# Moving the low part of a split from VectorE to TensorE and ScalarE in a Mamba scan (one core)

## What is computed

```python
A = -jnp.exp(A_log)
xp = jnp.einsum('bld,rd->blr', x, x_proj_w)
dt_in, B, C = ...
dt = jax.nn.softplus(jnp.einsum('blr,dr->bld', dt_in, dt_proj_w) + dt_proj_b)
dA = jnp.exp(dt[..., None] * A)
dBx = dt[..., None] * B[:, :, None, :] * x[..., None]
def step(h, inp):
    dA_t, dBx_t, C_t = inp
    h = dA_t * h + dBx_t
    y = jnp.einsum('bdn,bn->bd', h, C_t)
    return (h, y)
y = ys + D * x
```

## Time and profile before

| what | value |
|---|---|
| time, median of 3 runs | 844.35 us (841.13, 844.35, 847.69) |
| the profiled execution's own time | 841.76 us |
| its span in the profile | 840.0 us |
| busy in the span: PE / DVE / ACT / POOL | 779.4 / 620.4 / 439.4 / 307.7 us |
| the scan stage, from the first scan to the sum of the last product | 26.85 to 194.96 us |

### The profile page before, as it was taken

The page is one execution under the profiler, slowest core; times in us unless marked ns, Lnnn a source line. Parts: engine busy times, 40 slices in busy tenths (PEclk is TensorE's granted clock), DMA queues, the critical chain, the costliest instruction groups (busy, mean ns, idle before and its releaser), DMA issues.

```text
span 840.0 us, 18994 instructions
## 1 busy us (share of the span) xinstructions
PE 779.4 (93%) x7930; PEld 368.7 (44%) x7930; DVE 620.4 (74%) x879; ACT 439.4 (52%) x594; POOL 307.7 (37%) x235
## 2 busy tenths in 40 slices
PE   8758787797999999999999999999988999999997
PEld 2434344445444444444343444444424544444444
DVE  3999999997565333456759999999966787774344
ACT  4987767645754330143237788788895533332100
POOL 0799898992003000058402223222342122221000
PEclk9599999999999999999999999999999999999999
DMA  6900000005230000039900000000052033310011
GB/s 215 387 4 2 4 3 2 4 4 176 100 112 8 1 0 1 1 57 194 151 1 2 2 3 3 2 2 2 23 164 62 1 119 126 120 63 0 13 38 51
DMA packets 53296, 46.62 MB, mean 56 GB/s; under 512 B 38289, under 2 KB 44241, under 8 KB 53218
## 3 DMA queue, kind: packets, MB, share of 16 engines
q1 hardware_dynamic: 53218, 45.49, 18.8%
HBM read 34.87 MB, written 2.16 MB: 44 GB/s over the span
## 4 chain that ended last, share of the span: by engine, by line
PE 70%; DVE 15%; issue 5%; ACT 5%; POOL 2%; DMA 1%; SPq 1%; DVEq 0%; ACTq 0%; POOLq 0%
PE ps L906 13%; PE ps L670 10%; PE ps L647 9%; PE ps L828 8%; DVE arena L1462 7%; PE ps L942 7%; PE ps L749 6%; PE ps L726 6%; PE ps L805 4%; DVE arena L1686 2%; PE ps L753 2%; PE ps L561 1%; POOL arena L1296 1%; PE ps L515 1%; ACT arena L1195 1%
## 5 line engine op out<-in xcount | busy, mean ns | idle before, releaser
L1686 DVE TENSOR_REDUCE arena<-ps 128x1 f16<-128x512 f32 (+3 forms) x320 | 183.4, 630 | 16.6 <-PE ps L749 8.0
L1195 ACT ACTIVATE arena<-ps 128x1024 f32<-128x1024 f32 (+2 forms) x160 | 143.6, 942 | 36.6 <-PE ps L805 33.7
L1296 POOL TENSOR_TENSOR arena<-arena 128x1024 f32<-128x1024 f32 x62 | 145.5, 2377 | 12.1 <-DVE arena L1462 10.0
L1462 DVE TENSOR_TENSOR_SCAN arena<-arena,ps 128x1024 f32<-128x1024 f32 x64 | 141.9, 2270 | 0.8 <-PE ps L561 0.5
L906 PE MATMUL ps<-arena 128*128 128x512 f16 x528 | 114.6, 379 | 0.1
L670 PE MATMUL ps<-arena 128*128 128x512 f16 (+1 forms) x464 | 97.6, 372 | 1.0 <-ACT arena L1115 1.0
L749 PE MATMUL ps<-arena 64*128 64x512 f16 (+3 forms) x384 | 91.8, 329 | 3.3 <-DVE arena L1686 1.3
L561 PE MATMUL ps<-arena 64*128 64x64 f16 x3072 | 58.9, 194 | 33.5 <-DVE arena L1462 32.7
L647 PE MATMUL ps<-arena 128*128 128x512 f16 x384 | 88.8, 383 | 0.0
L561 PEld LDWEIGHTS ps<-arena 64*128 64x128 f16 x3072 | 51.1, 97 | 82.7 <-DVE arena L1462 78.2
L1354 POOL TENSOR_SCALAR_AFFINE_SELECT arena<-arena 128x512 f32<-128x512 f32 x64 | 42.0, 664 | 123.1 <-ACT arena L1195 122.9
(11 more groups left out here) (180 smaller groups left out, 968.9 us busy)
## 6 DMA issues: line engine op xcount, KB each, us to landing
arena<-in_w_q_dram SPq DMA_DIRECT2D x11, 768.0 KB, 4.1
arena<-c_rows SPq DMA_DIRECT2D x16, 512.0 KB, 10.7
arena<-in_w_s_dram SPq DMA_DIRECT2D x11, 384.0 KB, 4.9
arena<-in_x_fm_dram SPq DMA_DIRECT2D x8, 256.0 KB, 4.4
out_dram<-arena SPq DMA_DIRECT2D x8, 256.0 KB, 2.0
arena<-in_wg_dram SPq DMA_DIRECT2D x1, 1792.0 KB, 10.2
arena<-in_wu_dram SPq DMA_DIRECT2D x1, 1792.0 KB, 7.3
arena<-in_wd_dram SPq DMA_DIRECT2D x1, 1792.0 KB, 11.3
```

What stands on the lines that cost most here:

```text
L1195: nc.scalar.activation(dst, src, ACT.Exp, scale=float(HD) ** -0.5).then_inc(exp_done, 1)
L1296: nc.gpsimd.tensor_tensor(hC[i % 4][:], hst[i % 3][:], c_all[:, n, :], ALU.mult).then_inc(hc_done, 1)
L1462: nc.vector.tensor_tensor_scan(hst[i % 3][:], dA[i % 3][:], banks(2 * (i % 2), 2), 0.0, ALU.mult, ALU.add).then_inc(scan_done, 1)
L1686: nc.vector.reduce_max(maxima_slot(half, k), ps[:, ring_bank(n), 0:len(heads) * w].rearrange("p (a w) -> p a w", a=len(heads)), AX, negate ...
```

## The change

PE subtracts the high part from the turned product by a matmul with a negated identity in f16, accumulating in PSUM (`cut_high`: two matmuls of 128 x 512, behind the sum of n = 12, in chunk 0 of n = 13), and ACT copies what is left to f16 (`tok_low`, now on ACT, behind dA of n = 13, in chunk 0 of n = 14); DVE's `tok_low` is gone. For chunks 2 and 3, `make_dt` part 2 on DVE is gone too: PE adds max(z, 0) by a matmul with the f32 identity (`add_positive`: two matmuls of 128 x 512, behind the sum of n = 9), once part 1 has signalled. Chunk 1 keeps part 2 on DVE. The negated identity takes the place of `ident_h` and is made by one DVE instruction near the start. The transposes carry a start flag only on the first of the four in a bank.

```diff
--- before.py
+++ after.py
@@ -168,6 +168,7 @@
         picks_b = small("picks_b", [P, 2, P], bf16)
         b_parts = [x[:].rearrange("p s n -> p (s n)").bitcast(f32).rearrange("p (q n) -> p q n", q=TT) for x in (mask_b, picks_b)]
         ident_h = small("ident_h", [P, P], f16)
+        negative = ident_h
         skips = small("skips", [P, DC, SUB])
         ld_tab, tables_made = sem("ld_tab"), sem("tables_made")
         q_proj, k_proj, v_proj = sem("q_proj"), sem("k_proj"), sem("v_proj")
@@ -345,6 +346,7 @@
         b_kept, b_turned, b_high, diag_built, ident64_made = (
             sem("b_kept"), sem("b_turned"), sem("b_high"), sem("diag_built"), sem("ident64_made"))
         b_low, b_copied = sem("b_low"), sem("b_copied")
+        negative_made, tok_cut, log_joined = sem("negative_made"), sem("tok_cut"), sem("log_joined")
         diag_by_act, diag_by_pool = sem("diag_by_act"), sem("diag_by_pool")
         ACT_PIECES = {2: (6, 0), 3: (6, 1), 4: (8, 0), 5: (8, 1), 8: (11, 0), 9: (11, 1), 10: (14, 0), 11: (14, 1)}
         POOL_PIECES = {1: (7, 0), 3: (7, 1), 5: (12, 0), 7: (12, 1), 9: (15, 0), 11: (15, 1)}
@@ -528,8 +530,28 @@
                 if c:
                     pe.wait_ge(dt_done, whole(c))
                 for q in qs:
-                    last = nc.tensor.transpose(ps[:, TURN_BANK[c] + q // 4, (q % 4) * P:(q % 4 + 1) * P], dtx[:, q * P:(q + 1) * P], ident_sb[:])
+                    last = nc.tensor.matmul(ps[:, TURN_BANK[c] + q // 4, (q % 4) * P:(q % 4 + 1) * P], dtx[:, q * P:(q + 1) * P], ident_sb[:],
+                                            start=(q % 4 == 0), stop=True, is_transpose=True, skip_group_check=True)
                 last.then_inc(dtx_turned, 1)
+
+            def add_positive(c):
+
+                pe.wait_ge(log_joined, c - 1)
+                pe.wait_ge(z_pos, c)
+                for h in range(2):
+                    last = nc.tensor.matmul(banks(DT_BANK[c] + h, 1), ident_sb[:], dtx[:, h * HALF:(h + 1) * HALF],
+                                            start=False, stop=True, skip_group_check=True)
+                last.then_inc(dt_joined, 1)
+
+            def cut_high(c):
+
+                pe.wait_ge(tok_high_done, whole(c))
+                pe.wait_ge(negative_made, 1)
+                for h in range(2):
+                    last = nc.tensor.matmul(banks(TURN_BANK[c] + h, 1), negative[:],
+                                            dtx_tok[c % 2][:, 0, 4 * h:4 * h + 4, :].rearrange("p q d -> p (q d)"),
+                                            start=False, stop=True, skip_group_check=True)
+                last.then_inc(tok_cut, 1)
 
             def residual(c):
 
@@ -591,6 +613,10 @@
                     for lag in SUM_LAGS[c > 0].get(n, (LAG,)):
                         if i >= lag:
                             add_y(i - lag)
+                    if c + 1 < DC and n == (12 if c else 13):
+                        cut_high(c + 1)
+                    if 1 <= c < DC - 1 and n == 9:
+                        add_positive(c + 1)
             for n in range(NS - LAG, NS):
                 add_y((DC - 1) * NS + n)
 
@@ -1001,6 +1027,11 @@
 
                 act.wait_ge(dtx_turned, whole(c))
                 nc.scalar.copy(dtx_tok[c % 2][:, 0].rearrange("p q d -> p (q d)"), banks(TURN_BANK[c], 2)).then_inc(tok_high_done, 1)
+
+            def tok_low(c):
+
+                act.wait_ge(tok_cut, c)
+                nc.scalar.copy(dtx_tok[c % 2][:, 1].rearrange("p q d -> p (q d)"), banks(TURN_BANK[c], 2)).then_inc(tok_low_done, 1)
 
             def take_y(c):
 
@@ -1062,6 +1093,8 @@
                         keep_dt(c + 1)
                     if c + 1 < DC and n == (12 if c else 13):
                         tok_high(c + 1)
+                    if c + 1 < DC and n == (13 if c else 14):
+                        tok_low(c + 1)
             act.wait_ge(y_added, NS * DC)
             for h in range(2):
                 nc.scalar.copy(xT[0:SUB, DC - 1, h * HALF:(h + 1) * HALF], ps[SUB * h:SUB * h + SUB, 6, :]).then_inc(y_taken, 1)
@@ -1387,6 +1420,7 @@
             nc.vector.memset(dt_in[2 * NS:4 * NS, :], 1.0).then_inc(consts_made, 1)
             dve.wait_ge(ld_small, 4 * 16)
             nc.vector.tensor_tensor(ident64[:], ident_sb[:, 0:SUB], ident_sb[:, SUB:P], ALU.add).then_inc(ident64_made, 1)
+            nc.vector.tensor_scalar(negative[:], ident_sb[:], -1.0, None, ALU.mult).then_inc(negative_made, 1)
             nc.vector.tensor_scalar(dskip_sb[:], dskip_sb[:], 1.0, None, ALU.add).then_inc(consts_made, 1)
             dve.wait_ge(ident64_made, 1)
             dve.wait_ge(consts_made, 6)
@@ -1444,7 +1478,12 @@
                     own.done(nc.vector.scalar_tensor_tensor(joined(c), squares(c), 13.0 / 16, e_[:], ALU.add, ALU.mult))
                 elif part == 1:
                     dve.wait_ge(softlog, 2 * whole(c))
-                    own.done(nc.vector.tensor_tensor(joined(c), joined(c), log_e[:], ALU.min))
+                    if c == 1:
+                        own.done(nc.vector.tensor_tensor(joined(c), joined(c), log_e[:], ALU.min))
+                    else:
+                        nc.vector.tensor_tensor(joined(c), joined(c), log_e[:], ALU.min).then_inc(log_joined, 1)
+                elif part == 2 and c > 1:
+                    pass
                 elif part == 2:
                     dve.wait_ge(z_pos, c)
                     nc.vector.tensor_tensor(joined(c), joined(c), dtx[:], ALU.add).then_inc(dt_joined, 1)
@@ -1476,12 +1515,6 @@
                     dve.wait_ge(hc_done, i)
                     dve.wait_ge(y_added, i - 3)
                     nc.vector.tensor_tensor(hC[i % 4][:], hst[i % 3][:], c_all[:, n, :], ALU.mult).then_inc(hc_done, 1)
-
-            def tok_low(c):
-
-                dve.wait_ge(tok_high_done, whole(c))
-                rest, high = (dtx_tok[c % 2][:, s].rearrange("p q d -> p (q d)") for s in (1, 0))
-                nc.vector.tensor_tensor(rest, banks(TURN_BANK[c], 2), high, ALU.subtract).then_inc(tok_low_done, 1)
 
             def first_low(k):
 
@@ -1506,8 +1539,6 @@
                     part = n - (6 if c else 7)
                     if c + 1 < DC and 0 <= part < 4:
                         make_dt(c + 1, part)
-                    if c + 1 < DC and n == 13:
-                        tok_low(c + 1)
             last_products()
             take_last()
 
```

## The result

The changed kernel takes 836.77 us (median of 6 runs, 835.33 to 837.2) against 843.15 us before (median of 6, 840.89 to 847.69): 0.9914 of the time, 95% interval 0.9888 to 0.994. The profiled execution is at 835.33 us, before at 841.76; its span is 6.4 us shorter. A run of the same kernel again gave 0.993 (0.9909 to 0.9951).

A forecast was written before the change was run, and what follows sets the result against it. DVE was taken to bound the scan stage, with POOL next; 4 x 1.11 + 0.54 = 4.98 us saved gives 836.8 us from the profiled execution or 839.3 from the median, middle 838.0, range 833.5 to 844.0.

The forecast's parts named there:

- DVE first, POOL next: Scan stage: of 41.00 us per chunk DVE works 40.68 and POOL 38.02, so DVE savings count until POOL stops them.
- 4 x 1.11: Subtractions of chunks 0 and 1, adds of chunks 1 and 2: each removal from DVE shortens the stage by 1.11 us.
- 0.54 for the last subtraction: Chunk 2, before POOL's last run: of 1.11 us saved on DVE only POOL's wait of 0.54 us counts.
- the 2.0 that it called free: Scan stage: POOL's product may lag 2.0 us before a scan waits for the product three steps back.
- The f32 add at 2.24 us: PE, behind the sum of n = 9: two f32 matmuls take 2.24 us, hidden with 0.3 us to spare.
- The subtraction on PE and the copy on ACT cost nothing: End of each chunk: f16 matmuls of 0.43 to 0.76 us and a copy of 1.01 us fit into gaps.
- POOL's waits of 2.97 and 3.70 us against savings of 2.22: POOL up to 102.89 us, then to 144.02: its waits have room for DVE's saving of 2.22 us in each stretch.
- rival 1: POOL products from 102.89 us on slow to 2.36 us as scans close up: 1.5 us lost, gain 3.5; chance 0.15.
- The signs named: Profile after: adjacent scans, DVE busy some 6 us less, some 20 products in POOL's last run, stage end about 5 us earlier.
- 5 x 1.11 = 5.55: Three subtractions and two adds taken off DVE at 1.11 us each: 5.55 us of DVE time.
- The time: Whole kernel: 838.0 us, range 833.5 to 844.0; within one per cent 0.80, faster 0.16, slower 0.04.
- two anchors: Starting times for the whole-kernel forecast: profiled execution 841.76 us, giving 836.8, and median of runs shown 844.35, giving 839.3.

The follow-up runs named there:

- The doubled add: The changed kernel with each add of max(z, 0) in chunks 2 and 3 issued twice on PE; the scan stage took 166.57 us.
- the adds alone: Against the kernel before, only the two adds moved to PE, all subtractions staying on DVE; 0.9968 of the time, scan stage 167.66 us.

## Why the prediction was right, step by step

- *DVE first, POOL next.* Right. DVE's time came back until POOL stopped it. The whole gain without a fall of the clock is 5.05 us, the forecast's sum 4.98. That the two agree to 0.07 is in part luck: the single terms are off by -0.11, +0.16, +0.02, +0.16 and -0.16 us, and these cancel.
- *4 x 1.11.* Near: 1.00, 1.27, 1.13 and 1.27 us. The adds were worth more because the forecast counted the instruction and not the wait in front of the next one. VectorE waited for its own minimum before it went on, some 0.13 us, and that wait went to PE with the add. The subtraction of chunk 0 gives 1.00 without the fall of the clock and 0.08 in the profile with it; that TensorE's clock could fall there was not in the working at all. The estimate from the Trainium skill (Perfetto Trace Analysis, "Optimizing Scalar/DVE Operations"), 1.08 us each, and the row's 1.11 are both under the 1.13 measured for the subtraction of chunk 1 and for an add without its wait; the row's is the nearer.
- *0.54 for the last subtraction.* Right in kind, as the run with it back on DVE shows, but 0.36 to 0.38 in size, because DVE's own last products now start 0.2 us later behind POOL. The working had asked whether a scan comes to wait for the product three steps back, for 13 scans in a row, and had found it just inside. At the end of the stage 22 stand in a row (21 + 1 in the timeline of DVE), 21 x 0.14 = 2.9 us against the 2.0 that it called free, and there the scans do wait.
- *The f32 add at 2.24 us.* 1.98, with 0.49 us of room where 0.3 was forecast. The doubled add shows the room from the other side, 1.72 - 1.18 = 0.54.
- *The subtraction on PE and the copy on ACT cost nothing.* Right: 0.60 us in the range of 0.43 to 0.76, and in the profiles without a fall no scan waits for a dA behind the copy.
- *POOL's waits of 2.97 and 3.70 us against savings of 2.22.* Right: without a fall of the clock 0.79 and 0.71 + 0.78 = 1.49 us are left (the changed kernel again), where 2.97 - 2.22 = 0.75 and 3.70 - 2.22 = 1.48 were worked out. In the profile with the fall, in which the first saving hardly came, 0.87 + 0.78 = 1.65 are left at the first place. POOL did not get slower (rival 1); that rival counted 38 products, but the earlier trace rows have 36 from 102.89 on, so that its price would have been 1.4 us and not 1.5.
- *The signs named.* DVE's busy time fell by 5.3 us (615.1 after), where some 6 were named; 5 x 1.11 = 5.55 would have been nearer. The others came: scans side by side, 20 products in POOL's last run, the f32 matmuls under 2.5 us, no wait of DVE's product for ACT, and a stage shorter by more than 4 us.
- *The time.* The forecast of 838.0 us was 1.2 above the measured median. That is in part luck: it was the middle of two anchors 2.6 us apart, and in the profile the fall of the clock took 0.9 us from the gain in the stage while 2.3 us outside the stage, which the change did not make, added to it. The mechanism is borne out by the stage, not by this number.

## What to carry to other kernels

When one engine is full and the next is 93% full, list the second engine's waits ahead of time: their sum up to each point is what can be taken off the first engine there, and behind the last of them only its own last wait counts. An operation that is moved off the engine takes along the wait for its input that the engine did before it. Whether two profiles differ by the change or by chance is seen by a second profile of both, cut at the same instructions; here it was a fall of TensorE's clock that came and went in either kernel. And a wait that is put down to one engine is worth checking against the order of the work: the scan at 66.16 stood there as waiting for ACT, and it was PE that ended last.

## What was not expected of the hardware

TensorE's granted clock fell, from 2.4 to 1.2 GHz for most of 4 us (0.50 to 0.65 in windows of 2 us), at the same place, 62 to 66 us, in four of ten profiles, one of the kernel before among them. The gaps of PE in front of it were 1.42 to 1.55 us in every step, and the same gaps stood there in the profiles without a fall. The four are those in which the clock had been at 1.00 for some 3 us already near 30 us. The stretch from 400 to 420 us had a mean of 0.91 in seven of the ten and 1.00 in three, and these three are among the four. The fall at 62 to 66 us is worth 0.57 us before and 0.94 us after the change, nearly as much as one moved instruction, and the one at 112 to 118 us in the profile of the adds alone 1.5 us.
